# Routed layers that start on half of the tokens, and an attention projection ahead of the last zone product

## The reference

```
x = x + 0.5 * moe(norm(x))          # "f0": routed layer
x = x + attn0(norm(x))              # "a0": 16 heads of 8, 4 key heads
x = x + 0.5 * moe(norm(x))          # "f0" again, same weights
x = x + 0.5 * zones(norm(x))        # "f1"
x = x + attn1(norm(x))              # "a1": latent attention, 8 heads
x = x + 0.5 * zones(norm(x))        # "f1" again

moe:   scores = softmax(x @ gate_w.T); w = scores kept for the best 2 of 8, else 0
       out = sum_e w_e * (silu(x @ g_e) * (x @ u_e)) @ d_e              # e of width 176
             + sigmoid(x @ sg) * (silu(x @ gs) * (x @ us)) @ ds         # shared, width 352
zones: per sequence, tanh router on its mean picks 3 of 8 zones, widths 128-512-128, gelu;
       x + weighted sum
```

## Time and profile before

| | us |
|---|---|
| median of 3 runs | 1480.92 (1480.69 to 1482.76) |
| profiled execution | 1483.31 |
| its span | 1481.5 |
| first routed stage: head / loop | 18 to 54.5 / to about 297 |
| second routed stage: head / loop | 615 to 650 / to about 896 |
| join of zones and second attention | about 1062 to 1100 |

### The profile page before, as it was taken

The page is one execution under the profiler, slowest core; times in us unless marked ns, Lnnn a source line. Parts: engine busy times, 40 slices in busy tenths (PEclk is TensorE's granted clock), DMA queues, the critical chain, the costliest instruction groups (busy, mean ns, idle before and its releaser), DMA issues.

```text
span 1481.5 us, 27557 instructions
## 1 busy us (share of the span) xinstructions
PE 1425.8 (96%) x9728; PEld 1154.8 (78%) x9728; DVE 1102.9 (74%) x2433; ACT 977.9 (66%) x1759; POOL 595.4 (40%) x580
## 2 busy tenths in 40 slices
PE   6999999999999999999999999999989999989998
PEld 6888888765666665688888877999867777769998
DVE  3766777688888888477777787687778888866765
ACT  5556666657777777755665667877546666667886
POOL 4466667610000000026666666767501111146674
PEclk8999999999999999999999999999999999999999
DMA  6000000000000000020000002000000000000000
GB/s 180 1 1 1 1 1 1 1 0 1 2 1 1 1 1 1 2 88 1 1 0 1 1 8 79 1 2 1 1 1 2 2 2 1 2 2 1 16 15 29
DMA packets 13320, 16.87 MB, mean 11 GB/s; under 512 B 768, under 2 KB 10496, under 8 KB 12928
## 3 DMA queue, kind: packets, MB, share of 16 engines
q1 hardware_dynamic: 13184, 15.11, 3.3%
HBM read 13.01 MB, written 2.10 MB: 10 GB/s over the span
## 4 chain that ended last, share of the span: by engine, by line
PE 85%; DVE 8%; ACT 3%; issue 3%; DMA 1%; POOL 1%; SPq 0%; DVEq 0%; POOLq 0%; ACTq 0%
PE PS L646 20%; PE PS L674 10%; PE PS L1781 9%; PE PS L1798 8%; PE PS L799 5%; PE PS L819 5%; PE PS L807 4%; PE PS L170 2%; PE PS L1183 2%; PE PS L778 2%; PE PS L1187 2%; PE PS L1158 2%; PE PS L1140 1%; PE PS L1168 1%; PE PS L1207 1%
## 5 line engine op out<-in xcount | busy, mean ns | idle before, releaser
L543 POOL TENSOR_TENSOR RR<-AR,RR 128x512 fp32r<-128x512 f32 x150 | 193.9, 1292 | 470.6 <-ACT RR L574 464.3
L610 ACT ACTIVATE AR<-PS 128x512 f32<-128x512 f32 x224 | 133.9, 598 | 164.9 <-PE PS L646 162.6
L512 DVE TENSOR_TENSOR AR<-AR,PS 128x512 f32<-128x512 f32 x224 | 153.3, 685 | 116.6 <-PE PS L646 113.9
L918 ACT ACTIVATE AR<-PS 128x512 f32<-128x512 f32 x256 | 152.4, 603 | 85.9 <-PE PS L807 85.1
L995 DVE TENSOR_REDUCE AR<-PS 128x2 f32<-128x512 f32 x256 | 172.0, 684 | 21.8 <-PE PS L799 20.9
L646 PE MATMUL PS<-XHI,WG 128*128 128x512 f32 x448 | 177.1, 395 | 0.0
L646 PE MATMUL PS<-XHI,WU 128*128 128x512 f32 x448 | 174.8, 390 | 0.9 <-DVE AR L512 0.7
L516 DVE TENSOR_TENSOR AR<-AR,PS 128x512 f32<-128x512 f32 x224 | 153.8, 687 | 8.1 <-POOL RR L543 0.5
L1876 ACT ACTIVATE PS<-PS 128x1024 f32<-128x1024 f32 x96 | 96.8, 1009 | 58.9 <-PE PS L1781 58.6
L1781 PE MATMUL PS<-XHI,SL 128*128 128x256 f32 x576 | 133.6, 287 | 2.1 <-DVE XTR L1945 2.1
L2053 POOL CAST SL<-ZW 128x1024 fp32r x96 | 100.1, 1043 | 85.7 <-PE PS L1798 85.1
(11 more groups left out here) (281 smaller groups left out, 3465.4 us busy)
## 6 DMA issues: line engine op xcount, KB each, us to landing
...
```

What stands on the lines that cost most here:

```text
L512: v.tensor_tensor(PRD[:, m % 2, :], SIL[:, m % 2, :], bank(2 + m % 2), ALU.mult).then_inc(S.prod, 1)
L543: g.tensor_tensor(HL[k % 3], GAT[:, m % 2, :], HH[k % 3].bitcast(F32), ALU.subtract).then_inc(S.h_lo, 1)
L610: act.activation(SIL[:, m % 2, :], bank(m % 2), ACT.Silu).then_inc(S.silu, 1)
L918: act.activation(PT[:, g % 2, k, 2 * jp:2 * jp + 2, :], bank(2 + m % 2).rearrange("p (j q) -> p j q", j=2), ACT.Exp, scale=SC0).then_inc(S ...
```

## The change

Three parts. First, the head of a routed stage handles chunks 0 to 3 only (`HALF`), and gates them alone. The up products of tiles 0 and 1 move ahead of the gate weights, and `keep_busy` there shrinks from 46 or 38 to 14. Chunks 4 to 7 are normed, turned, copied and gated inside the loop, at tile numbers written into `late_pe`, `late_act` and `late_dve`; their transposes and logits share bank 7, and so do their gate weights. GpSimd sets `G.split` twice, after the up weights and after the down weights. The sum's copy `ACC` gets a place of its own behind `H3`; as the weights of zone 6 come to lie there, that zone is split later.

Second, in the zone stage that leads to a1, everything behind the norm's transposes of sequence 13 is handed to a1 (`ZTAIL`). There `project(0)` comes first, into banks 0 and 1, then the down product of step 47, then the leftovers in slots of steps -2 and -1.

Third, the zone weights' loads wait for the second half of the gate (`w_all + 2`).

```diff
-        HIGHS = (0, 6, 7, 1, 2, 3, 4, 5)
-        POOL_LO = (6, 2, 7)
+        HIGHS = (0, 7, 1, 2, 3, 4, 6, 5)
+        POOL_LO = (7, 2, 6)
...
-        ACC = ar(o + 768, 512)
+        HALF = NC // 2
+        ACC = nc.alloc_sbuf_tensor_at("ACC", [P, 512], F32, offset=experts_at + 4 * (6 * MT0 * P + 2 * P + 1024))[:, :]
...
+        def turned_in(c):
+            return bank(c % 4 if c < HALF else 7)
+        def logits_in(c):
+            return bank(4 + c % 4 if c < HALF else 7)[:, 0:TPC * GC]
...
+        def turn_in(n, c):
+            S, D = ST[n], counts(n)
+            pe = nc.tensor
+            if c < HALF:
+                wait(pe, S.xlo, c - 3, D.xlo)
+            elif c == HALF:
+                pe.wait_ge(S.wt_lo, D.wt_lo + 2)
+            else:
+                pe.wait_ge(S.lg_dve, D.lg_dve + c)
+            if c == NC - 1:
+                pe.wait_ge(S.x_new, D.x_new + 1)
+            if on_act(n) < TPC and c < HALF:
+                pe.wait_ge(S.xn, D.xn + c + 1)
+            pe.wait_ge(S.xna, D.xna + c + 1)
+            for t in range(TPC):
+                last = pe.transpose(turned_in(c)[:, t * P:(t + 1) * P], XN[:, c % 2, t, :], ident)
+            last.then_inc(S.tr, 1)
+        def logits(n, c):
+            S, D = ST[n], counts(n)
+            pe = nc.tensor
+            pe.wait_ge(S.xt, D.xt + c + 1)
+            if c >= HALF:
+                pe.wait_ge(S.xlo, D.xlo + c + 1)
+            for t in range(TPC):
+                last = pe.matmul(logits_in(c)[:, t * GC:(t + 1) * GC], XTC[:, c % 2, t * P:(t + 1) * P], T.gw,
+                                 start=True, stop=True)
+            last.then_inc(S.lg_pe, 1)
+        def copies_in(n, c):
+            S, D = ST[n], counts(n)
+            act = nc.scalar
+            act.wait_ge(S.tr, D.tr + c + 1)
+            wait(act, S.lg_pe, c - 1, D.lg_pe)
+            act.activation(XTC[:, c % 2, :], turned_in(c), ACT.Copy).then_inc(S.xt, 1)
+            act.activation(XHI[:, c * 512:(c + 1) * 512], turned_in(c), ACT.Copy).then_inc(S.xhi, 1)
...
+        def gate_exps(n, h):
+            S, D, ts = ST[n], counts(n), half(h)
+            act = nc.scalar
+            act.wait_ge(S.p_max, D.p_max + h + 1)
+            act.activation(PR[:, ts], PR[:, ts], ACT.Exp).then_inc(S.p_exp, 1)
+            act.activation(SG[:, ts], LG[:, ts, E0], ACT.Exp, scale=-1.0).then_inc(S.p_exp, 1)
...
+        def wt_place(r):
+            return (bank(4 + 2 * r, 2), slice(r * 1024, (r + 1) * 1024)) if r < 2 else (bank(7), slice((r + 2) * 512, (r + 3) * 512))
+        def wt_turn(n, r):
+            S, D = ST[n], counts(n)
+            pe = nc.tensor
+            pe.wait_ge(S.w_all, D.w_all + (1 if r < 2 else 2))
+            o, at = wt_place(r)
+            if r in (2, 4):
+                pe.wait_ge(S.x_new, D.x_new + 3 + (r - 2) // 2)
+            if r in (3, 5):
+                pe.wait_ge(S.wt_lo, D.wt_lo + r)
+            for t in range(at.start // P, at.stop // P):
+                last = pe.transpose(o[0:NG0, t * P - at.start:(t + 1) * P - at.start], WALL[:, t, :], ident)
+            last.then_inc(S.wt_pe, 1)
...
+        def late_pe(n, c, m):
+            k = MT0 * c + m
+            for i, at in enumerate((1, 5, 10, MT0 + 8)):
+                if k == at:
+                    turn_in(n, HALF + i)
+            for i, at in enumerate((4, 8, 13, MT0 + 11)):
+                if k == at:
+                    logits(n, HALF + i)
+            for i, at in enumerate((3 * MT0 + 8, 3 * MT0 + 11, 4 * MT0 + 8, 4 * MT0 + 11)):
+                if k == at:
+                    wt_turn(n, 2 + i)
+        def late_act(n, c, m):
+            k = MT0 * c + m
+            for i, at in enumerate((2, 6, 11, MT0 + 9)):
+                if k == at:
+                    copies_in(n, HALF + i)
+            for i, at in enumerate((3, 7)):
+                if at <= k < at + TPC:
+                    normed_in(n, HALF + 2 + i, [k - at])
+            if k == 2 * MT0 + 2:
+                gate_exps(n, 1)
+            for i, at in enumerate((3 * MT0 + 9, 3 * MT0 + 12, 4 * MT0 + 9, 4 * MT0 + 12)):
+                if k == at:
+                    wt_high(n, 2 + i)
+        def late_dve(n, ch, c, m):
+            v = nc.vector
+            k = MT0 * c + m
+            for i, at in enumerate((3, 7, 12, MT0 + 10)):
+                if k == at:
+                    low(n, HALF + i)
+            for i, at in enumerate((5, 9, MT0, MT0 + 12)):
+                if k == at:
+                    logits_out(n, HALF + i)
+            if k == 2 * MT0:
+                gate_logits(v, n, ch, 1)
+            if k == 2 * MT0 + 2:
+                gate_share(v, n, ch, 1)
+            if k in (2 * MT0 + 5, 2 * MT0 + 9):
+                gate_best(v, n, ch, 1, (k - 2 * MT0) // 9)
+            if k in (2 * MT0 + 6, 2 * MT0 + 11):
+                gate_first(v, n, ch, 1, (k - 2 * MT0) // 11)
+            if k == 2 * MT0 + 13:
+                gate_weights(v, n, ch, 1)
+            for i, at in enumerate((3 * MT0 + 10, 3 * MT0 + 13, 4 * MT0 + 10, 4 * MT0 + 13)):
+                if k == at:
+                    wt_low(n, 2 + i)
...
+            keep_busy(pe, bank(3), 18 if n else 20)
+            for c in range(HALF):
                 if c > 0:
-                    keep_busy(pe, bank(c % 4), 4)
-                if on_act(n) < TPC:
-                    pe.wait_ge(S.xn, D.xn + c + 1)
-                pe.wait_ge(S.xna, D.xna + c + 1)
-                for t in range(TPC):
-                    last = pe.transpose(bank(c % 4)[:, t * P:(t + 1) * P], XN[:, c % 2, t, :], ident)
-                last.then_inc(S.tr, 1)
-
-            def logits(c):
-                pe.wait_ge(S.xt, D.xt + c + 1)
-                wait(pe, S.lg_dve, c - 3, D.lg_dve)
-                for t in range(TPC):
-                    last = pe.matmul(bank(4 + c % 4)[:, t * GC:(t + 1) * GC], XTC[:, c % 2, t * P:(t + 1) * P], T.gw,
-                                     start=True, stop=True)
-                last.then_inc(S.lg_pe, 1)
-
-            keep_busy(pe, bank(3), 18 if n else 20)
-            for c in range(NC):
-                turn(c)
+                    wait(pe, S.xlo, c - 3, D.xlo)
+                    keep_busy(pe, turned_in(c), 4)
+                turn_in(n, c)
                 if c > 0:
-                    logits(c - 1)
-            logits(NC - 1)
-            pe.wait_ge(S.xlo, D.xlo + NC)
-            keep_busy(pe, bank(0), 38 if n else 46)
+                    logits(n, c - 1)
+            logits(n, HALF - 1)
+            pe.wait_ge(S.xlo, D.xlo + HALF)
...
+            mine = range(on_act(n))
+            normed_in(n, 0, mine)
+            normed_in(n, 1, mine)
+            for c in range(HALF):
+                copies_in(n, c)
+                if c + 2 < HALF:
+                    normed_in(n, c + 2, mine)
+            normed_in(n, HALF, range(TPC))
...
+            gate_exps(n, 0)
+            normed_in(n, HALF + 1, range(TPC))
+            for r in range(2):
+                wt_high(n, r)
...
+            def gates(c, s):
+                pe.wait_ge(S.wt_lo, D.wt_lo + (c // 2 + 1 if c < HALF else c - 1))
+                wait(pe, S.gated, MT0 * c if s else MT0 * (c - 1) + SHARED, D.gated)
+                pe.matmul(bank(4 + s), SEL[:, s * P:(s + 1) * P], WTS[:, bass.ds(c * 512, 512)],
+                          start=True, stop=True).then_inc(S.w_pe, 1)
...
+            pe.wait_ge(G.split, 1)
+            up(0, 0)
+            up(0, 1)
+            pe.wait_ge(S.lg_dve, D.lg_dve + HALF)
+            keep_busy(pe, bank(7), 14)
+            for r in range(2):
+                wt_turn(n, r)
             for c in range(NC):
...
+        def projected(b):
+            return (bank(5), bank(4)) if b else (bank(0), bank(1))
...
+            g.wait_ge(S.zero, 1)
+            for b in (NB - 2, NB - 1):
+                next_power(g, n - 1, b)
...
+                if b == 0 and q == 0:
+                    pe.wait_ge(S.blank, 7)
+                    pe.wait_ge(ST[n - 1].sum, counts(n - 1).sum + NB)
...
-                    if m == 0 and far:
+                    if m == 0 and far and i > -2:
                         project(i + 2)
+                    if m == 3 and i == -2:
+                        Z.back(NB - 1)
+                    if m == 5 and i == -2:
+                        Z.next_turn(NB - 2)
+                    if m == 3 and i == -1:
+                        Z.next_turn(NB - 1)
...
+            Z = ZTAIL["pe"]
+            project(0)
+            Z.down(NZ - 1)
             for i in range(-2, NB):
                 step(i)
...
+                    if m == 0 and i == -2:
+                        ZTAIL["act"].sums(NB - 1)
...
+                    if m == 1 and i == -2:
+                        Z.next_copy(NB - 3)
+                        Z.stats(NB - 2)
+                    if m == 4 and i == -2:
+                        Z.normed(NB - 2)
+                        Z.add(NB - 1)
+                        Z.stats(NB - 1)
```

(11 more changed lines are left out.)

255 lines of the change are left out of this document (132 added, 123 removed).

## The result

The changed kernel takes 1483.97 us (median of 20 runs, one of which was disturbed and took 3369.05 us) against 1482.05 us for the kernel before on the same chip (20 runs): the ratio is 1.0015, with a 95% interval of 1.0008 to 1.0021. So it is about 2 us slower, where 1475.6 us, 5.3 us faster, had been predicted. By the bound of the prediction (0.2%, 3 us) this counts as no change, which had a chance of 0.31; the time lies outside the range.

What follows compares the result with a forecast made beforehand. TensorE was taken as the bound inside both routed loops. First routed stage +3.3, second -2.0 and join -6.6 sum to -5.3 us, off the median 1480.92: 1475.6 us, range 1470 to 1483.

Steps and rivals of the forecast that it cites:

- What bounds the kernel: Both routed loops: TensorE is the bound, so a microsecond of matmul added there costs a microsecond.
- First head: Start of first routed stage: first down product at 55.3 instead of 62.33, 7.0 us earlier (bounds 4.6 and 9.6).
- Second head: Start of second routed stage: first down product at 644.9 instead of 658.00, 13.1 us earlier.
- The rival with the fall of the clock: Second head: TensorE's clock falls there too after idling, costing 2 to 5, say 3 us: 1478.6; chance 0.20.
- step (1) and (2): Routed loops, bank 7: waits for chunk 4's logits (1.5 us) and chunk 5's transposes (1.0), 2.5 us a stage.
- Step (3): Tile 30 of each routed loop: second half's exponentials with two table loads cost 0.9 us (first stage) and 1.7 (second).
- moved work: Routed loops: transposes, logits and half the turned gate weights moved in on TensorE, 6.9 us per stage.
- The rival of a VectorE bound: Loops' first three chunks: VectorE becomes the bound through 19 deferred steps a stage, 9.5 us more, 1485.1; chance 0.08.
- the drain: Table loads in both routed stages: the skill's 1.38 us drain per load shows, 5.5 us more, 1481; chance 0.03.
- Join: Zone stage to second attention: head keys 8.9 us earlier, next projection 7.4, less 0.8: -6.6 us (bounds -3 and -9).

Runs made afterwards that it cites:

- the join alone: Kernel before with only the change's join part, both routed stages as before; run twice: 1475.4 us (ratio 0.9949) and 1475.16 us (0.9951).
- the routed stages alone: The change without its join part, so routed stages begin on half of the tokens and the join is as before: 1491.26 us, ratio 1.0057.
- both moves of the exponentials: Two runs on the changed kernel: second half's exponentials in tile 32 (1484.26 us), or in tile 31 with gate operations one to a tile (1480.08 us).
- the spread gate: Changed kernel with the second half's gate operations on VectorE about one to a tile over tiles 30 to 47: 1480.26 us, ratio 0.9981.
- the added GpSimd load: Changed kernel with 7 subtractions (128x512) added on GpSimd in the second routed stage's head: 1486.86 us in one execution.
- the run with both moves: Changed kernel with the second half's exponentials in tile 31 and its gate operations one to a tile over tiles 31 to 48: 1480.08 us, ratio 0.9978.
- the spaced run: Changed kernel with late transposes (tiles 2, 8, 13) and logits (6, 11, 16) of chunks 4 to 6 further apart: 1483.00 us, ratio 1.0003.
- the runs with padding ahead: Changed kernel, 46 multiplies before the first stage's up products, 24 behind the second's up tiles; behind the first's none (1480.15 us) or 10 (1482.12 us).

## Why the prediction was wrong

- **What bounds the kernel**: right. 7.0 us of TensorE work moved into a loop made it 7.0 longer, to a tenth of what the earlier trace rows gave.
- **First head**, -7.0: the size came out in these two traces, and so did the low clock (0.5 from 30 to 42). The size is partly luck. The same head of before has its first down product at 62.33, 61.30 and 60.36 us in the three traces of it (before, and the two of the join alone), and the clock was down for about 10, 7 and 0 us in it (last section); the changed head has it at 55.29, and at 55.67 to 57.45 in the five other traces with the same head (the routed stages alone, both moves of the exponentials, the spread gate and the added GpSimd load). The means are 61.3 and 56.2, so that the head gives about 5 us and not 7. And the parts did not come out: the gate was estimated at 0.34 us an operation and ready at 40.2. It was ready at 44.1, since GpSimd splits weights beside it. It only did not show, because the padding held back the gate weights until 46.8. (A small slip besides: 4 us at half clock add 2 us to 52.8, which is 54.8 and not 54.4.)
- **Second head**, -13.1: -12.2. The gate took what it should with GpSimd idle (0.29 us an operation). The rival with the fall of the clock came true here (0.5 in 644 to 648, up products at 0.63 in place of 0.39 us), with about 1 us. In the run with the spread gate the clock held in this head, and it was 13.3 earlier (649.75 - 658.00 - 5.05). That was the exception: of the seven traces with this head (14 multiplies) the clock fell in six, for 3 to 10 us, and in none of the three with the head of before. From the start of the last logits to the first down product it took 18.9 us where the clock held, 19.8 to 19.9 in the three where it fell for up to 7 us, and 21.5 in the run with both moves, where it fell for 10.
- **Waits for bank 7**, step (1) and (2), 2.5 us: 2.0 and 1.5 in tiles 4 and 5, and nothing in the later ones, as written. Shown by the spaced run.
- **Step (3) failed.** 0.9 and 1.7 us were set down for the second half's gate; it cost 1.88 + 1.78 = 3.7 us in the first stage and 1.88 + 2.47 = 4.4 in the second, 5.4 us above the 2.6 of the forecast. The sum and the trace are 5.2 apart: the other terms (bank 7 1.6 less, moved work and small differences in the loops 0.7 more, second head 0.9 and join 0.8 more, 1.0 less at the zones) nearly cancel. Two things were missing. I set the exponentials beside the SiLU and the products only, and did not go through what else ScalarE has queued behind them: the accumulator's copy in the next tile, which the down product waits for. And I summed VectorE's load (28.6 us in 29.9) with durations from a head in which GpSimd stood still. The trace of before had the hold already, in the first head, where GpSimd splits weights until 43.14: one gate operation of 0.90 us, which is 0.43 in the second head. This sum is no bound either: the run with the operations spread has the same operations and none of the waits of tiles 39 to 45.

```profile
41.24 0.90 DVE L446 TENSOR_TENSOR AR<-AR 128x256 f32<-128x256 f32 x1
```

- The rival of a VectorE bound was right in its mechanism, wrong in size and extent: not each of the 19 deferred steps costs 0.6 or 0.7 us, but held operations that stand two or three to a tile.
- **The table load**: 120.38 + 1.28 = 121.66 and the silu starts at 121.67; the drain did not show here either.
- **Join**, -6.6: -5.8 in the profiled execution, whose clock was down at 1082 to 1087 (the next projection at 1.06 in place of 0.59 us), and about -7 for the join alone. In the ten other traces with this join the clock is 1.0 there. The parts, 8.9 and 7.4 earlier, came out at 9.1 and 7.3 to 7.7. In the trace of before the clock was down at 900 to 910 too (0.66), and with it goes the 1.0 us that the changed kernel gains between the second loop and the end of the zones. No part of the change gave it: from the last down product to the first projection it takes 170.7 us in the changed kernel's trace, where the clock held, and 172.2 in four others with the changed stages and in both of the join alone, where the clock fell for some 3 us.

On step (3) the Trainium skill bears (SBUF — State Buffer, Who interferes with whom), and I had not weighed it: it says that a VectorE instruction with two inputs in SBUF contends with a GpSimd instruction that reads SBUF, that copies and tensor_scalar can do so too in their modes that use both ports, and that a reduction on trn2 never does; whoever comes second is blocked until the other ends. The rows of this case agree: 0.57 to 1.35 us in place of 0.29 for tensor_tensor, 0.28 for the reductions, 0.69 for products with an operand in PSUM, and 1.28 in place of 0.18 for a copy of 16 elements.

The last 2 us, between traces and medians, are only partly settled. More of the span at the low clock goes with them (mean 0.990 against 0.995), the runs with padding ahead (0.995) are faster, and the traces name two places: the first head of before, late by 1 to 2 us in its own trace, and the fall in the second head, which most traces of the changed head have. What each costs on average was not measured.
